# Expert stage of a decoder layer: a new order of each round, gates as scales of the row products, one ring of tokens

## What is computed

```python
def _L0_ffn_ref(x, Wq, keys, W_in, W_out, in_a, in_b, out_a, out_b):
    q = (x @ Wq.T).reshape(b, n, 2, HEADS, DIM_KEY).transpose(2, 0, 1, 3, 4)
    sim = jnp.einsum('pbnhd,hkpd->pbnhk', q, keys)
    ...
    scores, pk = lax.top_k(all_scores, TOPK)             # TOPK = 1
    indices = jnp.take_along_axis(all_indices, pk, axis=-1)
    gate = jax.nn.relu(scores)
    hidden = x @ W_in.T                                   # 512 -> 1024
    lin = jnp.einsum('bnd,bnhkd->bnhk', x, in_a[indices]) * gate
    hidden = hidden + jnp.einsum('bnhk,bnhkd->bnd', lin, in_b[indices])
    hidden = jax.nn.gelu(hidden, approximate=False)
    out = hidden @ W_out.T                                # 1024 -> 512
    lout = jnp.einsum('bnd,bnhkd->bnhk', hidden, out_a[indices]) * gate
    out = out + jnp.einsum('bnhk,bnhkd->bnd', lout, out_b[indices])
```

## Time and profile before

| | |
|---|---|
| median of 3 runs | 2884.68 us (2881.69 to 2889.62) |
| profiled execution | 2886.98 us |
| its span | 2885.1 us |
| PE busy | 2485.5 us (86%) |
| DVE busy | 2157.1 us (75%) |
| ScalarE (ACT) busy | 1101.6 us (38%) |
| GpSimd (POOL) busy | 960.8 us (33%) |
| mean granted clock of PE | 0.948 |
| bytes read from HBM, written | 590 MB, 147 MB |

### The profile page before, as it was taken

How to read it: one execution, slowest core, us unless ns; L and a number is a source line. 1 busy time by engine, 2 the same in 40 slices (tenths; PEclk the granted TensorE clock), 3 DMA queues, 4 the chain that set the end, 5 groups by cost and what they waited for, 6 DMA issues and landing times. The chain is left out here.

```text
span 2885.1 us, 47969 instructions
## 1 busy us (share of the span) xinstructions
PE 2485.5 (86%) x12792; PEld 1361.4 (47%) x12792; DVE 2157.1 (75%) x6375; ACT 1101.6 (38%) x2559; POOL 960.8 (33%) x1486
## 2 busy tenths in 40 slices
PE   7889988899898998998858889888988889888885
PEld 4455555555555555555535334333433334333432
DVE  1567667666666766766533899999999999999997
ACT  2266666666566666666632111111111111111110
POOL 1133333333333333332312343334333443334342
PEclk9999999999999999999989999999999999999987
DMA  2034345444345444444458888889888988888886
GB/s 99 30 116 139 111 119 155 136 140 132 111 125 149 136 146 125 118 132 129 144 180 302 316 343 325 320 336 358 324 324 328 366 325 320 325 356 332 322 319 253
DMA packets 308544, 639.13 MB, mean 222 GB/s; under 512 B 163312, under 2 KB 168432, under 8 KB 308336
## 3 DMA queue, kind: packets, MB, share of 16 engines
q0 software_dynamic: 79616, 423.66, 37.5%
q1 hardware_dynamic: 194928, 112.31, 13.4%
q10 hardware_dynamic: 33792, 100.67, 10.5%
HBM read 590.38 MB, written 146.80 MB: 256 GB/s over the span
## 5 line engine op out<-in xcount | busy, mean ns | idle before, releaser
L1078 DVE CUSTOM_DVE_ANT_0 scores<-s_bank,added 128x512 f32<-128x512 f32 x512 | 350.7, 688 | 271.9 <-PE s_bank L581 190.0
L1419 PE MATMUL l_bank<-fold,xn_tf 128*128 128x512 f32 x1024 | 454.2, 597 | 40.3 <-ACT xn_tf L1482 24.7
L886 ACT ACTIVATE probs<-scores,nmx 128x512 f32<-128x512 f32 x512 | 372.7, 728 | 148.1 <-DVE nmx L1078 145.0
L1381 POOL DMA_INDIRECT out_rows<-rows_out,rows_now x256 | 258.7, 1010 | 507.2 <-DVE out_ps L1581 457.6
L892 ACT COPY prob_t<-t_bank 128x512 f32<-128x512 f32 x512 | 298.7, 584 | 208.9 <-PE t_bank L591 208.8
L519 POOL TENSOR_TENSOR added<-mask_add,band 128x136 f32<-128x136 f32 (+1 forms) x512 | 248.4, 487 | 360.3 <-DVE nmx L1078 359.0
L1372 POOL DMA_INDIRECT in_rows<-rows_in,rows_now x256 | 242.5, 947 | 272.7 <-PE hid_ps L1443 185.2
L1419 PEld LDWEIGHTS l_bank<-fold,xn_tf 128*128 128x128 f32 x1024 | 192.6, 191 | 278.2 <-issue 269.5
L591 PE MATMUL t_bank<-ident,probs 128*128 128x128 f32 x2048 | 314.5, 280 | 7.3 <-ACT cv L864 4.1
L591 PEld LDWEIGHTS t_bank<-ident,probs 128*128 128x128 f32 x2048 | 234.4, 142 | 178.1 <-issue 104.2
L1459 PE MATMUL out_ps<-w_out,hid_t 128*128 128x512 f32 x512 | 296.3, 743 | 22.1 <-ACT hid_t L1507 17.1
(11 more groups left out here) (176 smaller groups left out, 3665.9 us busy)
## 6 DMA issues: line engine op xcount, KB each, us to landing
rows_in<-in_in_b_dram ACTq DMA_DIRECT2D x16, 2048.0 KB, 9.3
rows_out<-in_out_a_dram ACTq DMA_DIRECT2D x16, 2048.0 KB, 9.2
rows_in<-in_in_a_dram ACTq DMA_DIRECT2D x16, 1024.0 KB, 5.5
rows_out<-in_out_b_dram ACTq DMA_DIRECT2D x16, 1024.0 KB, 5.5
x_scratch<-x SPq DMA_DIRECT2D x32, 512.0 KB, 7.5
rel_scratch<-rel_pad SPq DMA_DIRECT2D x16, 640.0 KB, 3.2
band<-rel_scratch SPq DMA_DIRECT2D x512, 20.0 KB, 2.1
prob_scratch<-probs SPq DMA_DIRECT2D x512, 20.0 KB, 2.4
```

The costliest lines, as they stand in the source:

```text
L886: nc.scalar.activation(prob_tile(s % PSLOTS), scores[:, s % 2, :], ACT.Exp, bias=nmx[:, s:s + 1], scale=-1.0, accum_out=lsum[:, s:s + 1]). ...
L1078: nc.vector.tensor_tensor_reduce(out=scores[:, s % 2, :], in0=s_bank[s % HPT][:, 0:L], in1=added[:, s % 2, :], scale=-1.0, scalar=-NEG, op ...
L1381: nc.gpsimd.indirect_dma_start(out_rows[:, h, :], None, rows_out, bass.IndirectOffsetOnAxis(rows_now[:, odd, h:h + 1], 0)).then_inc(out_lo ...
L1419: ins = nc.tensor.matmul(l_bank[c % 2][:], xn_t[:, k, :], fold[:, k, c * BANK:(c + 1) * BANK], start=(k == 0), stop=(k == KD - 1))
```

## The change

- **Order of a round.** Each engine now has a `step(r, slot)`. PE: chunks 0 to 2 of round r+2, the diagonal products of round r, chunk 3, the product with `W_in` of round r+1, only then the transposes of the gelu output of round r, the token transposes of round r+3, and the product with `W_out`. The product with `W_in` waits no more for the gelu but for the first sum in.
- **Sums.** The first sum in reads `hid_ps` and writes the SBUF tile `hid_sum`; the other five add up there, and gelu reads `hid_sum`. Of the sums out, heads 0 to 2 go to the SBUF tile `out_sum`, beginning with `x_res`, between the products out; heads 3 to 7 alternate between `out_ps` and `out_sum`, and a last addition joins the two. All drains but one are gone; in their place DVE waits for counts of its own instructions (`in_b_used`, `out_b_used`, `topped`, `searched`, `scored`), and finds and reductions stand between dependent sums.
- **Gates.** The row products take the gate as their scale, so the multiplications of `lin` and `lout` go, and the two copies of the gates; `gates` has two slots.
- **Search.** Four MAX8 of a chunk become one reduction with max over 4 x 128; the place is found with that one value, broadcast.
- **Tokens.** One load per round into a ring of four tiles (`xn_ring`) in place of two loads (`xn_pe`, `xn_ve`).
- **Loops.** The first four and the last four rounds are written out, and the loop's body holds four rounds, where it held one.

```diff
+        def rounds(step, eng):
+            for r in range(RING):
+                step(r, r)
+            with eng.Fori(1, ROUNDS // RING - 1) as i:
+                for j in range(RING):
+                    step(RING * i + j, j)
+            for r in range(ROUNDS - RING, ROUNDS):
+                step(r, r % RING)
...
-            def load_front(r):
-                wait(sp, xt_filled, r)
-                sp.sem_inc(gate, 1)
-                sp.dma_start(xn_pe[:], tokens(x3_dram, r)).then_inc(xpe_loaded, 16)
-
-            def load_products(r):
-                wait(sp, in_a_used, r * HEADS)
-                sp.sem_inc(gate, 1)
-                sp.dma_start(xn_ve[:], tokens(x3_dram, r)).then_inc(xve_loaded, 16)
+            def load_tokens(r, slot):
+                wait(sp, in_a_used, (r - RING + 1) * HEADS)
+                sp.sem_inc(gate, 1)
+                sp.dma_start(xn[:, slot, :], tokens(x3_dram, r)).then_inc(xn_loaded[slot], 16)
...
-                wait(pe, gelu_done, r)
+                wait(pe, in_b_used, (r - 1) * len(VE_HEADS) + 1)
                 for n in range(HALVES):
...
+            def step(r, slot):                       # PE
+                similarities(r + 2, range(0, 3))
+                heads_in(r)
+                similarities(r + 2, range(3, CHUNKS))
+                dense_in(r + 1)
+                turn_hidden(r)
+                turn_tokens(r + 3, (slot + 3) % RING)
+                dense_out(r)
...
-                nc.scalar.activation(hid[:], hid_ps[:], ACT.Gelu).then_inc(gelu_done, 1)
+                act.wait_ge(in_b_used, (r + 1) * len(VE_HEADS))
+                nc.scalar.activation(hid[:], hid_sum[:], ACT.Gelu).then_inc(gelu_done, 1)
...
+            def step(r, slot):                       # ScalarE
+                similarities(r + 2, range(0, 2))
+                diagonals(r)
+                similarities(r + 2, range(2, CHUNKS))
+                hidden(r)
+                keep(r + 2)
+                take_hidden(r)
+                take_tokens(r + 3)
...
-                    for g in pairs:
-                        nc.vector.max(top[:, g, :], sims[:, g * KEYS:(g + 1) * KEYS])
-                    self_wait(dve)
+            def largest(c):
+                nc.vector.tensor_reduce(top[:, c * PER:(c + 1) * PER],
+                                        sims[:, c * BANK:(c + 1) * BANK].rearrange("p (g k) -> p g k", k=KEYS),
+                                        AX.X, ALU.max).then_inc(topped, 1)
...
+            def sum_in(r, h):
+                if h == VE_HEADS[0]:
+                    dve.wait_ge(in_a_used, (r + 1) * HEADS)
+                    dve.wait_ge(hid_filled, r + 1)
+                else:
+                    dve.wait_ge(in_b_used, r * len(VE_HEADS) + h)
+                dve.sem_inc(gate, 1)
+                nc.vector.scalar_tensor_tensor(out=hid_sum[:], in0=in_b[:, h, :], scalar=lin[:, h:h + 1],
+                                               in1=hid_ps[:] if h == VE_HEADS[0] else hid_sum[:],
+                                               op0=ALU.mult, op1=ALU.add).then_inc(in_b_used, 1)
...
+            def sum_out(r, h):
+                dve.wait_ge(out_a_used, r * HEADS + h + 1)
+                in_bank = h >= FREE_OUT and (h - FREE_OUT) % 2 == 0
+                if h == 0:
+                    dve.wait_ge(xres_loaded, 16 * r + 16)
+                elif h == FREE_OUT:
+                    dve.wait_ge(out_filled, r + 1)
+                elif h < FREE_OUT:
+                    dve.wait_ge(out_b_used, r * HEADS + h)
+                else:
+                    dve.wait_ge(out_b_used, r * HEADS + h - 1)
...
+            def step(r, slot):                       # DVE
+                products_in(r, slot)
+                    search(r + 2, range(0, 1))
+                    largest(1)
+                    for i, h in enumerate(VE_HEADS):
+                        sum_in(r, h)
+                        if i < PER:
+                            find(PER + i)
+                        elif i == PER:
+                            largest(2)
+                    for g in range(2 * PER, 3 * PER):
+                        find(g)
+                    search(r + 2, range(3, CHUNKS))
+                product_out(r, slot, 0)
+                score_rows(r + 2)
+                for h in range(1, HEADS):
+                    product_out(r, slot, h)
+                    if h <= FREE_OUT:
+                        sum_out(r, h - 1)
+                pick(r + 2, slot)
+                for h in range(FREE_OUT, HEADS):
+                    sum_out(r, h)
+                finish(r)
```

More of the change, by code:

```diff
@@ L1179, in expert_pass @@
     SLOTS = HEADS
+    RING = 4
+    FREE_OUT = 3
     VE_HEADS = range(6)
@@ L1223, in expert_pass @@
         hid = sb("hid", [P, F])
+        hid_sum = sb("hid_sum", [P, F])
+        out_sum = sb("out_sum", [P, D])
         hid_t = sb("hid_t", [P, KF, P])
@@ L1339, in _ @@
             sp.dma_start(w_out[:], w["ffn_W_outT"].rearrange("(k p) n -> p k n", p=P)).then_inc(w_loaded, 16)
-            load_front(1)
-            load_front(2)
-            round_(0)
-            with sp.Fori(1, ROUNDS - 3) as r:
-                round_(r)
-            round_(ROUNDS - 3, ahead=False)
-            round_(ROUNDS - 2, ahead=False)
-            sp.wait_ge(res_ready, ROUNDS)
-            store(ROUNDS - 1)
+            for r in range(1, RING):
+                load_tokens(r, r)
+            rounds(step, sp)
             sp.wait_ge(res_stored, 16 * ROUNDS)
@@ L1421, in front, with dense_in @@
                     ins.then_inc(sims_filled, 1)
-                    if c == 1:
-                        within()
-            def back(r, beside):
+            def dense_in(r):
                 if isinstance(r, int) and r == 0:
@@ L1461, in back @@
                 ins.then_inc(out_filled, 1)
-            rounds(front, nothing, back, pe)
+            def step(r, slot):
+                if not nothing_after(r, 2):
+                    similarities(r + 2, range(0, 3))
+                heads_in(r)
+                if not nothing_after(r, 2):
+                    similarities(r + 2, range(3, CHUNKS))
+                if not nothing_after(r, 1):
+                    dense_in(r + 1)
+                turn_hidden(r)
+                if not nothing_after(r, 3):
+                    turn_tokens(r + 3, (slot + 3) % RING)
+                dense_out(r)
+            turn_tokens(0, 0)
+            similarities(0, range(CHUNKS))
+            dense_in(0)
+            turn_tokens(1, 1)
+            similarities(1, range(CHUNKS))
+            turn_tokens(2, 2)
+            rounds(step, pe)
         @block.scalar
@@ L1588, in _, with search, products_in @@
-            rounds(front, keep, back, dve)
+            def search(r, chunks):
+                for c in chunks:
+                    sims_full(r, c)
+                    largest(c)
+                    tops_known(r, c)
+                    for g in range(c * PER, (c + 1) * PER):
+                        if g == PH - 1:
+                            find_last(r)
+                        else:
+                            find(g)
+            def products_in(r, slot):
+                dve.wait_ge(xn_loaded[slot], 16 * filled(r, slot))
+                for h in (*PE_HEADS, *VE_HEADS):
+                    dve.wait_ge(in_loaded[h], 16 * r + 16)
+                    nc.vector.tensor_tensor_reduce(out=in_a[:, h, :], in0=in_a[:, h, :], in1=xn[:, slot, :],
+                                                   scale=gates[:, slot % 2, h:h + 1], scalar=0.0,
+                                                   op0=ALU.mult, op1=ALU.add,
+                                                   accum_out=lin[:, h:h + 1]).then_inc(in_a_used, 1)
@@ new lines, in product_out @@
+            def product_out(r, slot, h):
+                if h == 0:
+                    dve.wait_ge(gelu_done, r + 1)
+                dve.wait_ge(out_loaded[h], 16 * r + 16)
+                dve.sem_inc(gate, 1)
+                nc.vector.tensor_tensor_reduce(out=out_a[:, h, :], in0=out_a[:, h, :], in1=hid[:],
+                                               scale=gates[:, slot % 2, h:h + 1], scalar=0.0,
+                                               op0=ALU.mult, op1=ALU.add,
+                                               accum_out=lout[:, h:h + 1]).then_inc(out_a_used, 1)
@@ L1591, in decoder_layer @@
+            search(0, range(CHUNKS))
+            score_rows(0)
+            pick(0, 0)
+            search(1, range(CHUNKS))
+            score_rows(1)
+            pick(1, 1)
+            self_wait(dve)
+            rounds(step, dve)
 def decoder_layer(nc, w, out):
```

227 lines of the change are left out of this document (105 added, 122 removed).

## The result

| | us |
|---|---|
| before, median of 4 runs | 2885.49 (2881.69 to 2889.62) |
| after, median of 4 runs | 2764.93 (2760.35 to 2771.96) |
| ratio, 95% interval | 0.9584 (0.9558 to 0.9611) |
| profiled execution of after: time, span | 2771.96, 2770.0 |
| forecast, range | 2689, 2655 to 2780 |

The kernel is faster and inside the range, but of the 196 us forecast 121 came. The page of after: columns as on the page of before, first the engines, then the granted clock and the DMA rates in 40 slices, then the queue that carries instructions.

A forecast was written before the change was run, and what follows sets the result against it. DVE's instruction stream was taken to set the round; its terms summed to 34.7 us for 40.75. From 2884.68 us, 178.6 saved over 29 rounds and 17 beside them gave 2689 us, range 2655 to 2780.

The forecast's parts named there:

- products in, 8: DVE's row products into the round: 8 at 0.62 us, 4.96 us, with the gate as scale taken to cost nothing.
- search: DVE's search of four chunks: one reduction for four MAX8 each, 7.04 us for 8.39, 1.35 saved a round.
- sums in, 6: DVE's six sums in, to SBUF with other work between: 1.15 us each, 6.90 a round, saved 1.62.
- products out, 8: DVE's row products out of the round: 8 at 1.15 us, 9.20 us, gate as scale at no cost.
- sums out and closing: DVE's eight sums out and closing addition: five at 0.62, three at 0.70, closing 0.90; 6.10 us for 7.58.
- ahead of the rounds: Before the 29 rounds: PE no longer puts dense_in(0) behind the second search, saving 3 us.
- rounds 29 to 31: Last rounds, without search: the step from 39.3 to about 32 us (7 saved), the last two by 4 and 3.
- Instruction supply: Rival, chance 0.04: DVE's loop body of 366 instructions stalls 7.6 us each round; P = 42.3, 2909 us, slower.
- milder form: Rival, chance 0.05: DVE's instruction supply costs 1 to 3 us a round, giving 2720 to 2775 us.
- the 2.46 us of the rival: Rival, chance 0.02: each of POOL's 16 gather issues waits a DVE instruction, 1.24 + 1.22 us; 39.4 us, kernel 2825.
- the lower clock: Rival, chance 0.14: PE at the halved clock becomes the bound, needing 36.1 us a round; kernel 2730 us.
- the old spacing of the sums: Rival, chance 0.08: semaphore waits cost DVE what drains did, sums keep their spacing; P = 37.6, 2773 us.

The follow-up runs named there:

- e2: Changed kernel with scale 1.0 in place of the gates in both row products, gates left out of the computation; 2738.2 us, 0.9484 of before.
- e7: Changed kernel with a drain put back behind each sum in and each sum out; 2918.8 us, 1.0111 of before.
- e3: Changed kernel with PE's product with w_in moved back behind the gelu transposes and w_out product, ScalarE's copies following; 2979.6 us, 1.0326 of before.
- e5: Changed kernel with DVE's rounds written out and a third head's sum in moved from DVE to PE; 2736.5 us, 0.9485 of before.
- e4: Changed kernel with a loop body of two rounds, a ring of two token tiles and PE's second token load back; 2737.6 us, 0.9482 of before.

## Why the prediction was right or wrong

The 70 us of stage time that were forecast and did not come (195.6 against 1373.8 - 1247.9 = 125.9) are accounted for term by term. As in the prediction, the 29 rounds run from the first sum in of round 0 to that of round 29:

| term | forecast | measured | missing, us |
|---|---|---|---|
| products in, 8 | 4.96 | 5.38 | 0.42 a round |
| search | 7.04 | 7.10 | 0.06 |
| sums in, 6 | 6.90 | 7.11 | 0.21 |
| row numbers, gates | 0.50 | 0.53 | 0.03 |
| products out, 8 | 9.20 | 9.64 | 0.44 |
| sums out and closing | 6.10 | 6.10 | 0.00 |
| the round | 34.7 | 35.86 | 1.16, x 29 = 33.6 |
| jumps back | 0 | 26.3 + 3.8 | 30.1 |
| ahead of the rounds | 3 | 3.2 | -0.2 |
| rounds 29 to 31 | 14 | 7.8 | 6.2 |

These are 69.7. The other 6 us between 2689 and 2764.9 lie in the attention part and between single executions.

- *What bounds* was right: DVE sets the round before and after.
- *"That the scale is now read per partition costs nothing in the time per element, I take it; no row shows it"*: true of the single element, since 512 and 1024 cost the same, but the sum put the whole scale at nothing, the only term of the round without a row and without bounds. It costs 0.06 us in each of 16 products (e2), most of the round's 1.16 us. The edit still gains, 1.6 - 0.96 us a round.
- *Search, sums out, gates* came within 0.06 us each, and e7 bears out that the gain on the sums is other work in the place of a drain. *Sums in* went 0.035 us each over their nearest row.
- *Instruction supply* was a rival at 0.04, and 0.05 in the milder form, 1 to 3 us a round. The milder form came true in size, beside the forecast rather than in its place: 30.1 / 29 = 1.04 us a round. It came at five jumps, though, and not along the code. The grown loop body was the right thing to look at. The evidence used for and against it, and the straight-line rounds at the end, was about code in a row, and said nothing on jumps. The round of before is one loop body; its jumps cost nothing visible, and the text should have multiplied a bounded cost of a jump by the number of jumps. Its own list of what would be wrong has "issue" gaps of over 1 us on DVE in the loop, and five of 4.9 to 5.8 us came: on this point the mechanism failed.
- *PE* was right in its main points: the new order removes its chain (e3 shows the price), the clock stays up, the `w_out` product takes 7.13 us. Its wait before `h_bank` was forecast under 1 us and is 1.57, harmless slack as e5 shows. It is busy 33.02 us a round, 32.5 were forecast.
- *DMA* kept up, 0.94 busy at 373 GB/s; *POOL's* gather issues took 1.16 us (`in_rows`) and 1.05 us (`out_rows`) on the mean, far from the 2.46 us of the rival. The rule of the Trainium skill (SBUF — State Buffer, Who interferes with whom) on DVE instructions with two SBUF inputs shows in part: an issue takes 0.94 us beside a sum that reads PSUM, and mostly 1.15 to 1.48 us beside the sums in SBUF. That is a delay of some 0.2 to 0.5 us, and nobody waited for it.
- *Ahead of the rounds* came 3.2 us up to the first sum in (83.95 to 80.76 us from the first copy of `fold`), as forecast. `dense_in(0)` moved ahead of the second search; PE's wait of 5.97 us for `xn_tf` fell to 1.37, and that DVE stands 9.25 us for the second search costs nothing, since its first sum waits for PE even so.
- *Rounds 29 to 31* gained 7.8 of 14 us. With no search left, DVE waits 2.05 and 2.57 us for the diagonal products of the last two rounds, which take 5.10 and 5.62 us for the usual 3.70, after PE has stood 11.13 and 9.22 us. The prediction had no such wait.
- *Range and sign* held. For the range this was in part luck: its upper end was set by the lower clock and the old spacing of the sums, and neither came. Two other misses, of 34 and 30 us, took up most of that room.

## What to carry to other kernels

When a loop body is unrolled, count its instructions on each engine and put a price on each jump back: here 5 us once DVE's body was too long, none at half the length, so either stay short or write the loop out. A drain between dependent instructions is best replaced by a wait with other work in front of it, not by a wait alone. An operand that is read per partition in place of a constant has a price per instruction, so fold it into few instructions, not into all.

## What the runs showed of the hardware

- A jump back costs VectorE 4.9 to 5.8 us in after, where the body is 559 rows of the trace (4.1 to 6.9 in the other runs with a body of four rounds), 5.0 with 1116 rows, and nothing with 281. In the loops that stall, packets of instructions keep coming, and VectorE goes on 2.10 to 2.21 us after one has started. In the loops of before and e4, which do not stall, none come.
- Increments of a semaphore are not free beside the arithmetic: 160 of them added 5 to 6 us to a round, as waits between the products.
- "issue" in a row does not prove a lack of instructions. In after's first round DVE stands 4.49 us ahead of its sum at 1602.85, called "issue", and PE's diagonal products end at 1599.11 + 3.60 = 1602.71; in e5 the 0.85 us at 2134.44 is called so too, and PE ends at 2134.30.
- PE kept the upper clock behind waits of 0.99 and 1.57 us, and ran at the lower one behind 4.23, 6.02 and 6.74.
